# Attention values in eight blocks: two products a token group, halves joined by three engines

## The chip, the cores and the metric

The kernel runs on one core of a Trainium2 chip. A core has TensorE (PE in the profile; its weight loads are PEld), VectorE (DVE), ScalarE (ACT), GpSimd (POOL) and SyncE (SP), which only issues DMAs here. The metric is the device time of one launch in microseconds, the median of the runs shown; lower is better.

## The reference

Eight sequences of 1024 tokens and 256 channels pass through four sublayers, each followed by a residual and a layer norm. The third is the one that matters here: an attention in which each token attends over its own 16 heads.

```
q, k, v = qkv[..., :dh], qkv[..., dh:2*dh], qkv[..., 2*dh:]      # 16 heads of 16
scores = einsum('bnhd,bngd->bnhg', q, k) / 8
attn   = softmax(scores, axis=-1)
out    = einsum('bnhg,bngd->bnhd', attn, v)                      # the values
x      = out.reshape(b, n, -1) @ Wproj.T + bproj
```

The other sublayers are a linear attention with 1024 channels per sequence (a), a gated mixture of eight experts (the "moe" of a), and a feed-forward block on the 768 best tokens of each sequence (the router and ranking).

## The kernel before

The kernel is written engine by engine. Each engine has its own program, in which the order of the work is written out by hand in a function `turn(a, b, c)`; what one engine needs of another is a wait on a semaphore. A turn works on three sequences at once: a is in its first sublayer, b in the mixture of experts (`a_moe`, one call for each of eight token tiles), c in the head attention and the last sublayer. A turn lasts about 160 us. There are six turns with all three, at the start turns without c, and at the end one turn without a and one with c alone; so c's part runs eight times. An engine does its instructions strictly in the order of the turn.

Large numbers are kept as two fp16 parts, high (HI = 0) and low (LO = 1), with x = high + low. A product of two such numbers is the sum of three matmuls, `PASSES = ((HI, HI), (HI, LO), (LO, HI))`.

Tokens are handled in groups of eight (8 tokens x 16 channels of a head = 128 partitions). The matrix of one group is block-diagonal: `blockdiag` holds 128x128 fp16 weights for 16 groups and both parts. PE multiplies it with 16 columns. For the values (`b_o`) these columns are the transposed probabilities `probs_t`, which lie in the tile `ct`; the result of a group is 16 columns wide. Four steps q = 0 to 3 of 32 groups each fill a PSUM bank of 512 columns (O0 to O3). Per step PE does 32 x 3 = 96 matmuls, 384 a turn. PSUM banks for this part come from a ring of two (`b_bank`), so step q + 2 needs what step q left to be read.

After a step ScalarE rounds the bank to fp16 (the high part, 128x512, into `ohl`, which lies in the tile `stage`), and VectorE subtracts it from the bank (the low part, also into `stage`) and thereby frees the bank (`b_free`). When the last low part is there, SP and ScalarE issue four DMAs each to `scratch_o` in HBM; when all eight have landed SP issues two loads into `bt`, and from `bt` PE does the output projection (`b_pr`, weights `wproj`).

The order around it. On PE: `a_moe(b, 3)`, transposes of the probabilities (PT2, PT3), O0 to O3, then `a_tx(a, 0)`, `a_t(a, 0)`, `a_t(a, 1)`, `a_trow`, `a_tx(a, 1)`, `a_moe(b, 4)`, and then `b_pr(c, 0)`. On ScalarE: PT2, PT3, two block-diagonal copies (`b_spreadv(c, 1, ...)`), `a_moe(b, 3)` (four scaled copies), O0 to O3, `to_at_hi` of TX0, the stores of `b_storeo`, TX1. On VectorE: PT2, PT3, four block-diagonal products, O0 and O1, `a_moe(b, 3)` (four fused multiply-adds), O2 and O3, `a_tx(a, 0)`. On GpSimd: the scaling of the probabilities `b_s(c, 3)`, then `a_sum(b, 3)` (three additions) and the second layer norm's small steps.

Of the tile `prob` (128 x 2 x 512 fp32) nothing is needed once the last probabilities are transposed, until the router's scores.

## Time and profile before

| | |
|---|---|
| median of 3 runs | 1433.84 us (1431.96 to 1435.29) |
| the profiled execution | 1434.45 us, its span 1432.6 us |
| PE, PEld busy | 84%, 53% of the span |
| VectorE, ScalarE, GpSimd busy | 64%, 51%, 40% |
| mean granted TensorE clock | 0.855 of full speed |
| chain that ended last, by engine | PE 53%, DVE 18%, POOL 7%, issue 7%, DMA 6%, ACT 6% |

The chain is the work that set the end, followed back from the last instruction, step by step, to whatever released it. A wait of an engine counts only where that engine's next step lies on it.

### The profile page before, as it was taken

Reading aid. Unit: us, or ns where it says so; the run is one execution under the profiler, and the core shown is the slowest. Engines: PE = TensorE matmul, PEld = TensorE weight load, DVE = VectorE, ACT = ScalarE, POOL = GpSimd, SP = SyncE. Lnnn points to the kernel's source line nnn. Section 1 sums busy time; section 2 is a strip of 40 time slices with the busy share of each in tenths; the row PEclk is TensorE's granted clock in tenths of the full one; section 3 lists DMA queues with packets and bytes.
Section 4 is the critical chain, followed back from the end, with each engine's and each line's share of the span. In section 5 each row is a group of like instructions: output and inputs, shape, how many; then the busy total and the mean of one; then the engine's idle time right before and its main releaser. Section 6 shows DMA issues by size and latency. Waiting matters only on the chain.

```text
span 1432.6 us, 31148 instructions
## 1 busy us (share of the span) xinstructions
PE 1202.3 (84%) x12264; PEld 760.1 (53%) x12264; DVE 915.9 (64%) x2113; ACT 733.3 (51%) x1156; POOL 570.2 (40%) x887
## 2 busy tenths in 40 slices
PE   6689899997999899988999899988999898784443
PEld 3444456654665556654665556654665545442442
DVE  3534666587677866587677866587677776464534
ACT  3222465347554765357554675357454675356423
POOL 3125326425424525435424525435524515331312
PEclk8579998899879988899879987899879987787566
DMA  5000090205411190206410290207420290209220
GB/s 177 15 1 15 30 161 4 75 15 148 60 32 45 70 152 3 75 16 148 60 46 31 86 136 2 75 16 154 54 60 2 79 128 2 59 16 168 24 60 30
DMA packets 93145, 90.64 MB, mean 63 GB/s; under 512 B 7110, under 2 KB 81864, under 8 KB 92744
## 3 DMA queue, kind: packets, MB, share of 16 engines
q1 hardware_dynamic: 81736, 76.06, 26.8%
q0 software_dynamic: 2560, 8.39, 1.7%
q10 hardware_dynamic: 8704, 4.20, 1.1%
q8 instruction: 98, 1.61, 0.5%
q14 instruction: 47, 0.39, 0.1%
HBM read 46.68 MB, written 41.94 MB: 62 GB/s over the span
## 4 chain that ended last, share of the span: by engine, by line
PE 53%; DVE 18%; POOL 7%; issue 7%; DMA 6%; ACT 6%; SPq 2%; ACTq 1%; POOLq 0%; DVEq 0%
PE bank L1512 50%; DVE keys L1296 3%; POOL rs L521 2%; DVE x L1201 2%; DVE gelu L1298 2%; DVE stats L1060 2%; ACT x L793 1%; PE bank L1522 1%; DMA scratch_qkv<-part 1%; DMA scratch_qkv<-stage 1%; DMA bt<-scratch_o 1%; DVE ct L1030 1%; DMA scratch_o<-stage 1%; POOL stage L572 1%; DMA ct<-scratch_qkv 1%
## 5 line engine op out<-in xcount | busy, mean ns | idle before, releaser
L1512 PE MATMUL bank<-we,at 128*128 128x512 f16 x1536 | 365.5, 399 | 0.0
L1512 PEld LDWEIGHTS bank<-we,at 128*128 128x128 f16 x1536 | 154.0, 102 | 191.9 <-issue 36.4
L536 POOL TENSOR_TENSOR part<-part 128x512 f32<-128x512 f32 x64 | 83.0, 1297 | 353.8 <-ACTq L819 353.8
L671 ACT ACTIVATE part<-bank,wexp 128x256 f32<-128x256 f32 x256 | 105.2, 471 | 185.7 <-PE bank L1512 124.2
L1201 DVE SCALAR_TENSOR_TENSOR x<-bank,wexp,x 128x256 f32<-128x256 f32 x256 | 122.9, 480 | 81.0 <-PE bank L1512 75.0
L1512 PE MATMUL bank<-bt,wqkv 128*128 128x512 f16 x576 | 139.7, 385 | 15.6 <-DVE stage L1030 12.9
L793 ACT ACTIVATE x<-x,nm,rs 128x256 f32<-128x256 f32 x192 | 104.6, 593 | 92.5 <-POOL nm L524 91.2
L517 POOL TENSOR_SCALAR nm<-mv 128x2 f32<-128x2 f32 x128 | 32.3, 252 | 254.0 <-DVE mv L1065 248.5
L1030 DVE TENSOR_TENSOR stage<-bank,stage 128x512 f16<-128x512 f32 x112 | 75.6, 686 | 85.3 <-ACT stage L671 85.0
L1512 PE MATMUL bank<-keys,blockdiag 128*128 128x16 f16 x3072 | 96.6, 193 | 24.3 <-DMA keys<-scratch_qkv 18.5
L1512 PEld LDWEIGHTS bank<-keys,blockdiag 128*128 128x128 f16 x3072 | 95.6, 104 | 29.5 <-DMA keys<-scratch_qkv 19.0
L671 ACT ACTIVATE stage<-bank 128x512 f16<-128x512 f32 x112 | 66.2, 597 | 78.2 <-PE bank L1512 76.8
L1512 PE MATMUL bank<-ct,blockdiag 128*128 128x16 f16 x3072 | 82.9, 172 | 20.1 <-issue 20.0
L521 POOL TENSOR_TENSOR rs<-ve,half 128x2 f32<-128x2 f32 x128 | 95.3, 745 | 10.7
L1512 PEld LDWEIGHTS bank<-bt,wqkv 128*128 128x128 f16 x576 | 52.9, 99 | 83.9 <-DVE stage L1030 24.3
L1512 PEld LDWEIGHTS bank<-ct,blockdiag 128*128 128x128 f16 x3072 | 81.7, 101 | 22.6 <-issue 22.6
L1522 PE MATMUL bank<-const,x 128*128 128x128 f32 x384 | 59.6, 284 | 32.7 <-DVE ct L1030 15.9
L1030 DVE TENSOR_TENSOR ct<-bank,ct 128x512 f16<-128x512 f32 x64 | 41.6, 678 | 58.9 <-ACT ct L671 58.9
L671 ACT ACTIVATE blockdiag<-stage,const 128x2048 f16<-128x2048 f16 x40 | 78.1, 1994 | 0.0
L1060 DVE BATCH_NORM_STATS2 stats<-x 128x6 f32<-128x256 f32 x192 | 71.9, 416 | 8.7 <-POOL x L543 4.9
L572 POOL COPY stage<-ct 128x2048 f16<-128x2048 f16 x16 | 60.4, 3774 | 40.0 <-DMA ct<-scratch_qkv 39.9
L1522 PEld LDWEIGHTS bank<-const,x 128*128 128x128 f32 x384 | 45.7, 145 | 47.1 <-issue 21.5
(176 smaller groups left out, 2268.8 us busy)
## 6 DMA issues: line engine op xcount, KB each, us to landing
scratch_qkv<-stage SPq DMA_DIRECT2D x40, 512.0 KB, 3.8
ct<-scratch_qkv SPq DMA_DIRECT2D x128, 128.0 KB, 5.7
x_in<-in_x_dram SPq DMA_DIRECT2D x32, 256.0 KB, 2.7
keys<-scratch_qkv SPq DMA_DIRECT2D x64, 128.0 KB, 5.1
bt<-scratch_o SPq DMA_DIRECT2D x16, 512.0 KB, 3.7
out_dram<-x POOLq DMA_DIRECT2D x32, 256.0 KB, 2.7
scratch_qkv<-part SPq DMA_DIRECT2D x8, 512.0 KB, 8.2
scratch_o<-stage SPq DMA_DIRECT2D x32, 128.0 KB, 3.5
```

What stands on the lines that cost most here:

```text
L517: pool.tensor_scalar(nm[side][:, k, :], mv[side][:, k, :, 0], -1.0, None, ALU.mult)
L521: pool.tensor_tensor(rs[side][:, k, :], ve[side][:, k, :], half[:, 0:2], ALU.pow)\
L536: pool.tensor_tensor(part[:, 0:2, :], part[:, 0:2, :], part[:, 2:4, :], ALU.add)\
L572: pool.tensor_copy(v_rows[hf].rearrange("p (s c) h -> p s c h", c=8), compact[:, :, 8 * hf:8 * hf + 8, :]).then_inc(v_turned, 1)
L671: return act.activation(dst, src, ACT.Copy, scale=scale)
L793: ins = act.activation(dsts[t], srcs[t], ACT.Identity, bias=nm[side][:, k, t:t + 1], scale=rs[side][:, k, t:t + 1])
L1030: return dve.tensor_tensor(dst, src, hi, ALU.subtract)
L1060: ins = dve.bn_stats(stats[side][:, t, :], srcs[t])
L1201: ins = dve.scalar_tensor_tensor(out=dst, in0=m_bank[q][:, D * (e % 2):D * (e % 2 + 1)], scalar=wexp[:, t, e:e + 1], in1=dst, op0=ALU.mult ...
L1296: dve.tensor_scalar(beats_on[:, o:o + P * (T - 1 - t)], scores[:, P * (t + 1):C], me, None, ALU.is_le, ALU.add, accum_out=rowsum[:, t, 0:1])
L1512: ins = pe.matmul(dst, lhs, rhs, start=(n == 0), stop=(n == len(terms) - 1))
L1522: ins = pe.transpose(ps[:, 2 * P * k + P * t:2 * P * k + P * (t + 1)], src[:, 2 * p + t, P * k:P * (k + 1)], ident)
```

## The change

The bank of a step is now filled by 16 groups instead of 32, and a group takes two matmuls instead of three: one of the high weights with high and low probabilities together (32 columns), and one of the low weights with the high probabilities (16 columns), which adds to the first 16 of those. A group's result so lies in PSUM as two halves of 16 columns that have still to be added. There are eight steps n (O0 to O7) of 32 matmuls and 512 PSUM columns each.

The halves are joined in four steps. ScalarE copies the LO half (256 columns) from PSUM into one of four places in `prob` (`b_oextra`). VectorE adds the other half to it from PSUM, in place, and frees the bank (`b_o`). ScalarE rounds the sum to fp16 from `prob` into `ohl` (`b_o`). GpSimd subtracts that from the sum and writes the low part (`b_olo`). From n = 4 on ScalarE's first copy also waits for GpSimd to have read the place. The stores wait for GpSimd's eighth step.

On VectorE `a_moe(b, 3)` now stands between steps 3 and 4; on ScalarE copy n comes ahead of rounding n - 1; on GpSimd the eight steps stand ahead of `a_sum(b, 3)`.

```diff
-        def o_part(q, part):
-            return ohl[:, :, part, :].rearrange("p h (r c) -> p h r c", c=16)[:, :, :, 4 * q:4 * q + 4]
-
-        def o_psum(q):
-            return b_ps(f"O{q}").rearrange("p (c r h) -> p h r c", c=4, r=T)
+        def o_part(n, part):
+            return ohl[:, :, part, :].rearrange("p h (r c) -> p h r c", c=16)[:, :, :, 2 * n:2 * n + 2]
+
+        def o_products(n):
+
+            return b_ps(f"O{n}").rearrange("p (a l g) -> p l a g", l=2, g=H)
+
+        def o_half(n):
+            return prob[:, n // 2 % 2, 256 * (n % 2):256 * (n % 2 + 1)]
+
+        def o_sum(n):
+            return o_half(n).rearrange("p (c r h) -> p h r c", c=2, r=T)
...
-                sp.wait_ge(b_free[b_ring("O2")], b_read(b, "O2"))
-                sp.sem_inc(waits_held, 1)
-                sp.wait_ge(b_free[b_ring("O3")], b_read(b, "O3"))
+                sp.wait_ge(o_lo, 8 * (b + 1))
...
+            def b_olo(b, n):
+                pool.wait_ge(o_hi, 8 * b + n + 1)
+                pool.sem_inc(waits_held, 1)
+                pool.tensor_tensor(o_part(n, LO), o_sum(n), o_part(n, HI), ALU.subtract).then_inc(o_lo, 1)
...
                     b_s(c, 3)
+                    for n in range(8):
+                        b_olo(c, n)
                 if b is not None:
                     a_sum(b, 3)
                     ln(b, 5, 0)
...
-            def b_o(b, q):
-                act.wait_ge(b_full, b_filled(b, f"O{q}"))
+            def b_oextra(b, n):
+                act.wait_ge(b_full, b_filled(b, f"O{n}"))
+                if n >= 4:
+                    act.wait_ge(o_lo, 8 * b + n - 3)
+                copy(o_half(n).rearrange("p (a g) -> p a g", g=H), o_products(n)[:, LO]).then_inc(o_extra, 1)
+
+            def b_o(b, n):
+                act.wait_ge(b_free[b_ring(f"O{n}")], b_read(b, f"O{n}"))
                 for hf in range(2):
                     act.wait_ge(v_spread[hf], 2 * (b + 1))
-                copy(o_part(q, HI), o_psum(q)).then_inc(o_hi, 1)
+                copy(o_part(n, HI), o_sum(n)).then_inc(o_hi, 1)
 
             def b_storeo(b):
-                for q in (2, 3):
-                    act.wait_ge(b_free[b_ring(f"O{q}")], b_read(b, f"O{q}"))
-                    act.sem_inc(waits_held, 1)
+                act.wait_ge(o_lo, 8 * (b + 1))
+                act.sem_inc(waits_held, 1)
...
-                    b_o(c, 0)
-                    b_o(c, 1)
-                    b_o(c, 2)
-                    b_o(c, 3)
+                    b_oextra(c, 0)
+                    for n in range(1, 8):
+                        b_oextra(c, n)
+                        b_o(c, n - 1)
+                    b_o(c, 7)
...
-            def b_o(b, q):
-                dve.wait_ge(o_hi, 4 * b + q + 1)
-                split_lo(o_part(q, LO), o_psum(q), o_part(q, HI)).then_inc(b_free[b_ring(f"O{q}")], 1)
+            def b_o(b, n):
+                dve.wait_ge(o_extra, 8 * b + n + 1)
+                half = o_half(n).rearrange("p (a g) -> p a g", g=H)
+                dve.tensor_tensor(half, o_products(n)[:, HI], half, ALU.add).then_inc(b_free[b_ring(f"O{n}")], 1)
...
                     b_spreadv(c, 1, range(2, 6), last=True)
-                    b_o(c, 0)
-                    b_o(c, 1)
+                    for n in range(4):
+                        b_o(c, n)
                 if b is not None:
                     a_moe(b, 3)
                 if c is not None:
-                    b_o(c, 2)
-                    b_o(c, 3)
+                    for n in range(4, 8):
+                        b_o(c, n)
...
-            def b_o(b, q):
-                pe.wait_ge(v_spread[q // 2], 2 * (b + 1))
-                pe.wait_ge(b_free[b_ring(f"O{q}")], b_before(b, f"O{q}"))
-                pe.wait_ge(b_free[1 - b_ring(f"O{q}")], b_other(b, f"O{q}", (f"PT{q}",)))
-                for c in range(4):
+            def b_o(b, n):
+                pe.wait_ge(v_spread[n // 4], 2 * (b + 1))
+                pe.wait_ge(b_free[b_ring(f"O{n}")], b_before(b, f"O{n}"))
+                pe.wait_ge(b_free[1 - b_ring(f"O{n}")], b_other(b, f"O{n}", (f"PT{n // 2}",)))
+                for c in range(2):
                     for r in range(T):
-                        n = T * c + r
-                        ins = sum_of(b_ps(f"O{q}")[:, H * n:H * (n + 1)],
-                                     [(block(q, i, r, c),
-                                       probs_t[:, j, 4 * q + c, H * r:H * (r + 1)]) for i, j in PASSES])
+                        o, m = 2 * H * (T * c + r), 2 * n + c
+                        seen = probs_t[:, :, m, H * r:H * (r + 1)]
+                        pe.matmul(b_ps(f"O{n}")[:, o:o + 2 * H], block(HI, r, m), seen, start=True, stop=False)
+                        ins = pe.matmul(b_ps(f"O{n}")[:, o:o + H], block(LO, r, m), seen[:, HI, :],
+                                        start=False, stop=True)
                 ins.then_inc(b_full, 1)
 
             def b_pr(b, p):
```

## Rows read from the trace of the kernel before

**Rows 1.** Timeline of one of six full turns: start us, us, engine, line, work [idle]

```profile
568.82 3.89 ACT L671 ACTIVATE blockdiag<-stage,const 128x2048 f16<-128x2048 f16 x2
...
569.27 5.01 PE L1512 MATMUL bank<-ct,blockdiag 128*128 128x16 f16 x192 [1.02 <-issue]
...
572.60 1.56 ACT L671 ACTIVATE part<-bank,wexp 128x256 f32<-128x256 f32 x4
...
574.36 1.08 ACT L671 ACTIVATE stage<-bank 128x512 f16<-128x512 f32 x2 [0.19 <-PE bank L1512]
574.99 1.29 DVE L1030 TENSOR_TENSOR stage<-bank,stage 128x512 f16<-128x512 f32 x2 [2.58 <-ACT stage L671]
...
575.78 3.96 PE L1512 MATMUL bank<-ct,blockdiag 128*128 128x16 f16 x143 [1.51 <-issue]
576.20 2.03 DVE L1201 SCALAR_TENSOR_TENSOR x<-bank,wexp,x 128x256 f32<-128x256 f32 x4
...
581.57 0.60 ACT L671 ACTIVATE stage<-bank 128x512 f16<-128x512 f32 x1 [2.45 <-PE bank L1512]
...
582.20 0.69 DVE L1030 TENSOR_TENSOR stage<-bank,stage 128x512 f16<-128x512 f32 x1 [2.35 <-ACT stage L671]
...
582.52 0.60 ACT L671 ACTIVATE at<-bank 128x512 f16<-128x512 f32 x1 [0.35 <-PE bank L1522]
582.99 3.17 SPq L454 DMA_DIRECT2D scratch_o<-stage  x4
...
588.90 5.34 PE L1512 MATMUL bank<-we,at 128*128 128x512 f16 x24
...
594.09 0.55 PEld L1512 LDWEIGHTS bank<-wproj,bt 128*128 128x128 f16 x6 [0.34 <-DMA bt<-scratch_o]
```

**Rows 2.** Windows of it: stretch, us, busy PE PEld DVE ACT POOL, clock, DMA

```profile
569.27:574.30 5.03, 5.01 (x192) 4.91 (x192) 3.15 (x5) 4.90 (x6) 0.01 (x1) 0.93 0.01 3
575.80:581.50 5.70, 5.36 (x193) 5.29 (x194) 3.01 (x6) 0.60 (x1) 1.30 (x2) 0.50 0.03 6
```

**Rows 3.** Timeline, first projection work: six full turns (first, last), then the seventh

```profile
273.52 0.55 PEld L1512 LDWEIGHTS bank<-wproj,bt 128*128 128x128 f16 x6 [0.74 <-DMA bt<-scratch_o]
...
1075.24 0.57 PEld L1512 LDWEIGHTS bank<-wproj,bt 128*128 128x128 f16 x6 [0.29 <-DMA bt<-scratch_o]
...
1232.11 1.46 PE L1512 MATMUL bank<-wproj,bt 128*128 128x256 f16 x6 [6.13 <-DMA bt<-scratch_o]
```

**Rows 4.** Timeline of the last turn, in which c is alone

```profile
1356.39 10.43 PE L1512 MATMUL bank<-ct,blockdiag 128*128 128x16 f16 x384 [2.07 <-issue]
...
1359.65 0.60 ACT L671 ACTIVATE stage<-bank 128x512 f16<-128x512 f32 x1 [0.56 <-DVE blockdiag L1228]
...
1367.49 0.69 DVE L1030 TENSOR_TENSOR stage<-bank,stage 128x512 f16<-128x512 f32 x1 [1.87 <-ACT stage L671]
...
1379.17 1.25 PE L1512 MATMUL bank<-wproj,bt 128*128 128x256 f16 x5 [12.35 <-DMA bt<-scratch_o]
```

**Rows 5.** Groups by line and shape: busy us, mean ns of one, idle before

```profile
L671 ACT ACTIVATE blockdiag<-stage,const 128x2048 f16<-128x2048 f16 x40 | 78.1, 1994 | 0.0
...
L572 POOL COPY stage<-ct 128x2048 f16<-128x2048 f16 x16 | 60.4, 3774 | 40.0 <-DMA ct<-scratch_qkv 39.9
...
L539 POOL TENSOR_TENSOR part<-part 128x256 f32<-128x256 f32 x64 | 47.3, 739 | 5.0
...
L530 POOL TENSOR_TENSOR xs<-x_in,xs 128x512 f16<-128x512 f32 x32 | 36.1, 1156 | 54.3 <-ACT xs L671 54.2
...
L671 ACT ACTIVATE shared<-ct 128x2048 f16<-128x2048 f16 x8 | 29.8, 3719 | 0.0
...
L565 POOL COPY x<-x 128x512 f32<-128x512 f32 x32 | 19.5, 612 | 7.6 <-DMA out_dram<-x 7.5
...
L1111 DVE TENSOR_TENSOR shared<-bank,iq 128x256 f32<-128x256 f32 x8 | 3.3, 417 | 0.0
...
L671 ACT ACTIVATE iq<-bank 128x256 f32<-128x256 f32 x8 | 3.1, 384 | 20.6 <-PE bank L1512 20.6
```

More of the change, by code:

```diff
@@ L38, in build_two_layer_postln @@
               "F10", "F11", "S0", "S1", "PT0", "S2", "PT1", "S3", "PT2", "PT3", "O0", "O1", "O2", "O3",
+              "O4", "O5", "O6", "O7",
               "PR0", "PR1", "PR2", "PR3", "TZ0", "TZ1", "TZ2", "TZ3", "ROUT0", "ROUT1", "SCOL0",
@@ L213, in build_two_layer_postln @@
         pt_hi = sem("pt_hi")
+        o_extra = sem("o_extra")
         o_hi = sem("o_hi")
+        o_lo = sem("o_lo")
         o_stored = sem("o_stored")
@@ L1658, in b_f, with block @@
                     .then_inc(b_full, 1)
-            def block(q, part, t, c):
-                return blockdiag[:, q // 2, 64 * part + 8 * t + 4 * (q % 2) + c, :]
+            def block(part, t, m):
+                return blockdiag[:, m // 8, 64 * part + 8 * t + m % 8, :]
             def b_s(b, q):
@@ L1673, in b_s @@
                         ins = sum_of(b_ps(f"S{q}")[:, H * n:H * (n + 1)],
-                                     [(block(q, i, g, c), keys[:, :, P * j + token])
+                                     [(block(i, g, 4 * q + c), keys[:, :, P * j + token])
                                       for i, j in PASSES])
@@ L1770, in turn @@
                     b_pt(c, 3)
-                    b_o(c, 0)
-                    b_o(c, 1)
-                    b_o(c, 2)
-                    b_o(c, 3)
+                    for n in range(8):
+                        b_o(c, n)
                 if b is None and c is None:
```

## The prediction

> **What bounds the kernel now.** I first looked at the granted clock and at the chain that ended last, which runs mostly through PE. The value products fill their stretch, so fewer of them look like time won. Whether that is so is decided by what starts the output projection, the first thing that needs the values. The timeline of a full turn answers it. PE begins the values at 569.27 and does 192 matmuls in 5.01 us, then stands until 575.78, because ScalarE is still busy with its block-diagonal copies (from 568.82) and with the four scaled copies of the experts (572.60 to 574.16), and reads the first bank only at 574.36 [rows 1]. The last low part ends at 582.20 + 0.69 = 582.89, the stores go out at 582.99, and the projection's first weights load at 594.09, 11.1 us later, after a wait of 0.34 us for the loads of `bt` [rows 1]. So the projection waits for DMA, not for PE, and the expert matmuls in front of it (5.34 us from 588.90 [rows 1]) just cover the transfers. It is the same in every turn: in the six full ones the wait is between 0.29 and 0.74 us (I show the first and the last), in the seventh, which has no a, it is 6.13 us [rows 3]; in the last nothing stands in front but the transfers. The end is therefore set, in all eight turns, by the moment at which the last low part of the values is in `stage`. PE's own time in the values is not what is late.
>
> **PE: 384 matmuls become 256.** The 192 matmuls take 26.1 ns each at a mean granted clock of 0.93, and 143 of the later ones 3.96 us, 27.7 ns each, in a stretch at 0.50, which is the 1.2 GHz level [rows 1, 2]. In the last turn 384 take 10.43 us, 27.2 ns each [rows 4]. The rate hardly follows the clock, so the 16 columns are not what limits them, and I take 27.4 ns also for the 32-column product: a step of 32 matmuls is 0.88 us. That removes 128 x 27.4 ns = 3.5 us of PE a turn, 28 us in all. No row has a 32-column product. Its bounds are 27.4 ns, and twice that if the columns counted, with the other half unchanged, which makes 1.3 us a step.
>
> **Prices of the joining.** ScalarE's copy of a half from PSUM is like the 128x256 copy of `iq`, 0.384 us; VectorE's addition is like the 128x256 product from PSUM, 0.417 us [rows 5]. ScalarE's rounding reads `prob` in jumps of 512 bytes, then 64. Nearest is its copy out of `ct`, in jumps of 256 bytes: 3719 ns against 1994 ns for as many elements read in a row, 0.84 ns more an element [rows 5]. With 256 elements that is 0.2 us on 0.4: I take 0.60, bounds 0.40 and 0.60. GpSimd's subtraction is bounded below by half of its 128x512 one to fp16, 1156 / 2 = 0.58 us; the nearest whole row is 0.739 us for 128x256 [rows 5]. It too reads in jumps: its copy out of `ct` takes 3774 / 2048 = 1.84 ns an element, the straight one 612 / 512 = 1.20, so 0.64 x 256 = 0.16 us more for one such operand and 0.33 for two [rows 5]. I take 0.74 + 0.16 = 0.90, bounds 0.58 and 1.10. Handing over costs 0.03 us from ScalarE to VectorE (582.17 to 582.20) and 0.10 from VectorE to PE or to a DMA issue (582.89 to 582.99) [rows 1].
>
> The same jumps are weighed by a rule. The Trainium skill, GPSIMD Engine Reference, section "Performance pitfalls for Q7 kernels", says that reading SBUF with steps above 8 bytes costs some 2.9 instead of 1.9 cycles an element; at its 1.2 GHz this is an estimate of 0.21 us for 256 elements. GpSimd would then take 0.95 us and the whole sum below would be 17.4 us instead of 16.2. It speaks against giving this work to GpSimd.
>
> **A full turn, step by step** (times on the clock of [rows 1]).
> Steps 0 and 1 are through PE at 571.0, since only their two banks are free. ScalarE does not come before 574.36: nothing of its work ahead of that is changed. It copies half 0 until 574.75 and half 1 until 575.05 (independent ones overlap a little, as the pair in 1.08 us shows [rows 1]). VectorE's first addition ends at 575.20, and PE resumes at 575.3, only 0.5 us earlier than now, with six of its eight steps still to do, where now it has half.
> From there the round PE, ScalarE, VectorE, PE paces it: step 2 ends at 576.2, 3 at 577.1, 4 at 578.1, 5 at 579.0. VectorE ends addition 3 at 578.0 and then does the experts' four operations, 2.03 us [rows 1], before addition 4 (580.4). The banks of 4 and 5 are held for that time; PE does step 6 from 580.5 and step 7 until 582.3, 0.7 us later than now.
> Then the tail: copy 7 until 582.7, addition until 583.2, rounding until 583.8. GpSimd's subtraction 6 runs from 583.3 to 584.2 and 7 until 585.1. Against 582.89 that is +2.25 us. Behind bank 7 there was one rounding and one subtraction, now there are four steps on three engines. The transfers take their 11.1 us as before, so the projection starts 2.25 us later. PE, which arrives 0.7 us later, is hidden by that.
> With the bounds it is +1.4 us (0.40 and 0.58) to +2.85 us (0.60 and 1.10).
>
> **What is queued behind the new waits.** On ScalarE, TX0 moves from 582.52 to about 583.8; PE's T0 matmuls, which do not need it, cover that. ScalarE's issue of stores waits for GpSimd with TX1 behind it, which PE delivers only after 588, so nothing is lost. On GpSimd, `a_sum(b, 3)` goes behind the eight subtractions: from 585.1, with additions of about 1.16, 0.74 and 0.74 us [rows 5], it ends near 587.9, and VectorE wants it for the norm's statistics after the T work, just about then; the cost is nothing as long as the subtractions end before 586, and after that VectorE's wait runs beside the transfers. SP's x loads go out behind the stores, 2 us later, for use in the next turn.
>
> **The seventh turn** has the same order, +2.25. **The last** has no expert work: PE is now continuous for 10.43 us from 1356.39, ScalarE is idle from 1359.09, and the end is 1367.49 + 0.69 = 1368.18 [rows 4]. With halves from 1359.1, additions from 1359.6 and a round of about 0.95 us a step, step 7 is through PE at 1365.7, 1.1 us earlier; the tail of 2.9 us ends at 1368.6: +0.4 (bounds -0.4 and +1.6).
>
> **Sum.** 7 x 2.25 + 0.4 = 16.2 us; bounds 7 x 1.4 - 0.4 = 9.3 and 7 x 2.85 + 1.6 = 21.6. After the projection every engine keeps its order and is behind it, so I take nothing back. The profiled execution took 1434.45 us, 0.6 above the median, so 1434.45 + 16.2 - 0.6 = 1450.
>
> **The rivals.**
> *PE's time is the gain.* If the projection followed PE's last value matmul, 8 x 3.5 = 28 us would go: 1406. For it speaks that PE is most of the chain; against it that the projection waits for DMA in all turns [rows 3] and that ScalarE reads nothing before 574.36. It decides from the point at which ScalarE's first copy comes before about 571.5, and nothing moves it there. Chance 0.04; a part of it, with a gain of over 3 us, 0.02.
> *No difference.* Later in the turn some wait that does not stem from c takes up the delay. At the lower bound, with most of it taken up, the result is 1434 to 1437. I saw no such wait. Chance 0.08.
> *GpSimd paces.* If one subtraction takes 1.3 us or more, eight of them from 575.9 end at 586.3, +3.4 a turn and +3.0 in the last: 1434 + 27 = 1461. Two operands in jumps point that way, the rows up to 1.1 do not reach it. A 32-column product at 1.3 us a step gives 3.9 a turn and 2.6 in the last, +30: 1464. Together 0.12.
> *The clock falls in the longer wait before the projection.* In the seventh turn, after 6.13 us of waiting, its first six matmuls take 1.46 us [rows 3]; were it so in the six full turns, over 1 us more each, near 1458. There PE would wait for some 1.8 us only. Chance 0.06.
> *The forecast*, 1443 to 1456: chance 0.68.
>
> **How the numbers follow.** The likeliest is 1450. The range, 1440 to 1461, holds the forecast, the clock's case, half of the pacing case and what lies between the forecast and no difference. A difference of about 0.2% (2.9 us) is what a measurement of this kernel can tell from none. Faster 0.06, same 0.08, slower 0.86.
>
> **What would show it.** Right: PE idle for over 4 us after 64 value matmuls; ScalarE's first half at the place of today's first rounding; stores some 2 us later after the start of the values, and the projection's wait for `bt` grown from 0.3 to about 1.8 us in full turns. Wrong: a subtraction on GpSimd outside 0.58 to 1.10 us, a step of PE over 1 us, a rounding from `prob` at 0.4 us (which takes 0.2 off a turn), or a projection that starts without waiting for its load.

## The result

The changed kernel takes 1459.48 us (median of 4 runs, 1454.47 to 1462.97), the kernel before beside it 1432.9 us (1430.16 to 1435.29): a ratio of 1.0183, 95% interval 1.0142 to 1.0225. The sign is as forecast; the size, 26 us, is not the 16 us of the sum. 1459 lies above the forecast's own 1443 to 1456, just inside the upper edge of the range of 1440 to 1461. The profiled execution took 1456.38 us with a span of 1454.6 us, 22.0 us more than the span before, at a mean granted clock of 0.864 (before 0.855).

The page of the kernel after: span, busy time by engine, and the chain that ended last.

```profile
span 1454.6 us, 29436 instructions
...
PE 1172.2 (81%) x11240; PEld 734.0 (50%) x11240; DVE 923.8 (64%) x2145; ACT 772.7 (53%) x1252; POOL 635.6 (44%) x951
...
PE 46%; DVE 17%; issue 10%; POOL 9%; DMA 8%; ACT 6%; SPq 2%; ACTq 1%; POOLq 0%; DVEq 0%
```

PE's share of the chain fell from 53% to 46%, while issue, GpSimd and DMA took its place. PE has less to do and waits more.

The groups of the changed value stage, by line and shape: count, busy us, mean ns of one, idle before and what ended it.

```profile
L592 POOL TENSOR_TENSOR stage<-prob,stage 128x256 f16<-128x256 f32 x64 | 62.0, 988 | 93.1 <-ACT stage L686 92.8
...
L686 ACT ACTIVATE stage<-prob 128x256 f16<-128x256 f32 x64 | 41.5, 657 | 9.0 <-DVE prob L1288 9.0
...
L1288 DVE TENSOR_TENSOR prob<-bank,prob 128x256 f32<-128x256 f32 x64 | 25.8, 422 | 44.2 <-ACT prob L686 43.1
L686 ACT ACTIVATE prob<-bank 128x256 f32<-128x256 f32 x64 | 23.7, 383 | 9.4 <-PE bank L1717 8.6
```

The copy (383 ns) and the addition (422 ns) cost what their nearest rows of before did, 384 and 417 [rows 5]. The two operations that read `prob` in jumps cost more than I took: 657 ns for the rounding against 600, 988 ns for the subtraction against 900, though this one is inside its bounds.

The timeline of the same full turn as in [rows 1], after: start us, us, engine, line, work, idle before. PE's rows come in pairs of lines for 32 and 16 columns; the first of a run stands.

```profile
574.32 0.18 PE L1716 MATMUL bank<-ct,blockdiag 128*128 128x32 f16 x1 [1.02 <-issue]
...
577.65 1.56 ACT L686 ACTIVATE part<-bank,wexp 128x256 f32<-128x256 f32 x4
...
579.33 0.66 ACT L686 ACTIVATE prob<-bank 128x256 f32<-128x256 f32 x2
...
580.27 0.19 PE L1716 MATMUL bank<-ct,blockdiag 128*128 128x32 f16 x1 [4.20 <-issue]
...
582.92 2.03 DVE L1222 SCALAR_TENSOR_TENSOR x<-bank,wexp,x 128x256 f32<-128x256 f32 x4
...
587.59 0.38 ACT L686 ACTIVATE prob<-bank 128x256 f32<-128x256 f32 x1
...
587.85 2.85 POOL L592 TENSOR_TENSOR stage<-prob,stage 128x256 f16<-128x256 f32 x3 [0.48 <-ACT stage L686]
...
588.00 0.42 DVE L1288 TENSOR_TENSOR prob<-bank,prob 128x256 f32<-128x256 f32 x1 [0.43 <-ACT prob L686]
...
590.80 3.26 SPq L462 DMA_DIRECT2D scratch_o<-stage  x4
...
601.88 0.55 PEld L1534 LDWEIGHTS bank<-wproj,bt 128*128 128x128 f16 x6 [0.97 <-DMA bt<-scratch_o]
```

From the first value matmul to the first store this turn takes 590.80 - 574.32 = 16.48 us; before it took 582.99 - 569.27 = 13.72 [rows 1]. Read down: PE does its two banks and then stands 4.20 us (before 1.51 [rows 1]), because ScalarE first does the scaled copies of the experts; the experts on VectorE at 582.92 hold the banks of steps 4 and 5; and the last copy at 587.59 is followed by an addition (588.00) and a rounding, while GpSimd does the last three subtractions in a row from 587.85 on, the last of which ends at 590.70.

Put together over all eight turns, from both timelines:

| | before | after | difference, us |
|---|---|---|---|
| first value matmul to first store, seven turns, sum | 93.4 | 115.1 | +21.7 |
| the same in the last turn | 11.88 | 12.65 | +0.8 |
| first store to projection, eight turns, sum | 90.2 | 92.2 | +2.0 |
| projections, sum | 53.8 | 58.6 | +4.8 |
| from a projection to the next turn's values, and before the first | | | -7.4 |
| span | 1432.6 | 1454.6 | +22.0 |

In this sum the stage itself gives all of it, +3.1 us a turn. The projections' +4.8 us and the -7.4 us nearly cancel, and 1.8 us of the latter lie before the first value matmul of the program, where nothing was changed. The section on the prediction comes back to both.

### The profile page after: what moved, and what is told of

Read it like the earlier page. It is cut to its first block, busy times and chain, and to the rows that moved or that the text cites. A ratio compares the mean times of both kernels' runs of the same rounds, so it can differ in the third digit from the quotient of the medians.

```text
span 1454.6 us, 29436 instructions
## 1 busy us (share of the span) xinstructions
PE 1172.2 (81%) x11240; PEld 734.0 (50%) x11240; DVE 923.8 (64%) x2145; ACT 772.7 (53%) x1252; POOL 635.6 (44%) x951
## 4 chain that ended last, share of the span: by engine, by line
PE 46%; DVE 17%; issue 10%; POOL 9%; DMA 8%; ACT 6%; SPq 2%; ACTq 1%; POOLq 0%; DVEq 0%
PE bank L1534 41%; DVE keys L1318 3%; PE bank L1716 2%; POOL rs L529 2%; DMA bt<-scratch_o 2%; DMA scratch_o<-stage 2%; DVE x L1222 2%; DVE gelu L1320 2%; ACT x L813 1%; POOL stage L592 1%; DVE stats L1081 1%; ACTq L783 1%; DVE ct L1051 1%; DMA scratch_qkv<-part 1%; DMA scratch_qkv<-stage 1%
## 5 line engine op out<-in xcount | busy, mean ns | idle before, releaser
L1534 PE MATMUL bank<-bt,wqkv 128*128 128x512 f16 x576 | 137.5, 380 | 16.6 <-DVE stage L1051 13.7
L592 POOL TENSOR_TENSOR stage<-prob,stage 128x256 f16<-128x256 f32 x64 | 62.0, 988 | 93.1 <-ACT stage L686 92.8
L1716 PE MATMUL bank<-ct,blockdiag 128*128 128x32 f16 x1024 | 58.4, 185 | 52.2 <-issue 51.1
L1544 PE MATMUL bank<-const,x 128*128 128x128 f32 x384 | 59.7, 285 | 32.7 <-DVE ct L1051 16.2
L1534 PE MATMUL bank<-wproj,bt 128*128 128x256 f16 x384 | 57.7, 300 | 33.8 <-DMA bt<-scratch_o 33.8
L1716 PEld LDWEIGHTS bank<-ct,blockdiag 128*128 128x128 f16 x1024 | 55.8, 102 | 55.6 <-issue 55.6
L1051 DVE TENSOR_TENSOR stage<-bank,stage 128x512 f16<-128x512 f32 x80 | 54.2, 685 | 40.2 <-ACT stage L686 40.0
```

The source lines that it names most:

```text
L592: pool.tensor_tensor(o_part(n, LO), o_sum(n), o_part(n, HI), ALU.subtract).then_inc(o_lo, 1)
L1051: return dve.tensor_tensor(dst, src, hi, ALU.subtract)
L1534: ins = pe.matmul(dst, lhs, rhs, start=(n == 0), stop=(n == len(terms) - 1))
L1544: ins = pe.transpose(ps[:, 2 * P * k + P * t:2 * P * k + P * (t + 1)], src[:, 2 * p + t, P * k:P * (k + 1)], ident)
L1716: pe.matmul(b_ps(f"O{n}")[:, o:o + 2 * H], block(HI, r, m), seen, start=True, stop=False)
```

## The experiments

The change has three parts: steps of a quarter of the work that a bank held before (eight half-filled blocks instead of four), two matmuls a group instead of three, and the joining of the halves. The first two experiments take the parts one by one; the others test which neighbour of the stage makes it slow. "Stage" below is the time from the first value matmul to the first store in a full turn: 13.2 to 13.7 us before, 16.4 to 16.5 after. The rows shown are those of the third full turn, as above.

**Only the smaller blocks.** Three products of 16 columns a group as before, in eight steps; ScalarE rounds each half bank, VectorE subtracts. Nothing is left out.

```
def o_first(n):
    return b_ps(f"O{n}")[:, 0:256].rearrange("p (c r h) -> p h r c", c=2, r=T)
# ScalarE
copy(o_part(n, HI), o_first(n)).then_inc(o_hi, 1)
# VectorE
split_lo(o_part(n, LO), o_first(n), o_part(n, HI)).then_inc(b_free[b_ring(f"O{n}")], 1)
```

> Block size alone: the three products of the kernel before (384 matmuls a turn) in eight steps of 16 groups, ScalarE rounding and VectorE subtracting 256 columns straight from PSUM; VectorE's expert operations between steps 3 and 4 as in the changed kernel. Nothing is left out. Theory 1: a step is 1.32 us of PE, only two steps (not half the work) are done when ScalarE arrives, and VectorE's expert operations hold two banks, so the stores go out 15.3 to 15.8 us after the first value matmul (before 13.2, without the joining 14.3): about 1449, so that the block size alone costs more than two thirds of what the change cost. If block size is harmless, 13.2 to 13.6 and 1434 to 1437.

Measured: 1461.51 us (1460.49 to 1467.44), ratio 1.0217 [1.0181, 1.0252]. The stage takes 15.99 us in every full turn and 13.33 in the last. Timeline of its PE, ScalarE, VectorE and ScalarE's queue:

```profile
575.24 2.56 PE L1521 MATMUL bank<-ct,blockdiag 128*128 128x16 f16 x96 [1.02 <-issue]
...
590.28 0.40 ACT L682 ACTIVATE stage<-bank 128x256 f16<-128x256 f32 x1 [0.87 <-PE bank L1521]
...
590.71 0.42 DVE L1039 TENSOR_TENSOR stage<-bank,stage 128x256 f16<-128x256 f32 x1 [0.85 <-ACT stage L682]
...
591.38 3.48 ACTq L774 DMA_DIRECT2D scratch_o<-stage  x4
```

The tail behind PE is short, 590.28 to 591.13, and yet the whole loss is there. The cause is in front: two banks now hold a quarter of the values instead of half, so PE does 96 of its 384 matmuls, a quarter, before it must wait for a late ScalarE (the first row; before it did 192 [rows 1]), and its value part lasts 15.0 us. I had priced this too low: 15.3 to 15.8 us for the stage and about 1449 in all. PE's value part, 3.2 us longer than before, also brings PE to the projection as late as the loads: its weight loads wait only 0.12 to 0.40 us there in five of the six full turns. The smaller block alone costs as much as the whole change does.

**Two products, no joining.** The low-probability half of each product is left out of the values; `o_first` is then the first half of the products; ScalarE rounds it straight from PSUM, VectorE subtracts, GpSimd has nothing to do here.

```
# ScalarE
copy(o_part(n, HI), o_first(n)).then_inc(o_hi, 1)
# VectorE
split_lo(o_part(n, LO), o_first(n), o_part(n, HI)).then_inc(b_free[b_ring(f"O{n}")], 1)
```

> PE's part of the change without the joining: the same 256 matmuls in eight steps, but ScalarE rounds the first half straight from PSUM and VectorE subtracts it there, as before; the half with the low probabilities is left out of the values. Theory 1 (the stores wait for ScalarE's arrival and for the chain behind the last bank, PE's time in the values is not on the path): from the first value matmul to the stores 13.3 to 14.0 us, as before (13.2), time within +0 to +6 us of the kernel before. Theory 2 (PE's saved 3.5 us a turn count and the joining hides them): about 9.8 us to the stores and 1405 us.

Measured: 1443.26 us (1442.82 to 1446.28), ratio 1.0043 [1.0028, 1.0059]. The stage takes 14.3 us, a little over the 13.3 to 14.0 expected, and 11.10 in the last turn. Timeline, PE, VectorE and SP's queue:

```profile
574.31 0.18 PE L1703 MATMUL bank<-ct,blockdiag 128*128 128x32 f16 x1 [1.02 <-issue]
...
588.12 0.43 DVE L1039 TENSOR_TENSOR stage<-bank,stage 128x256 f16<-128x256 f32 x1 [0.42 <-ACT stage L682]
...
588.64 3.54 SPq L465 DMA_DIRECT2D scratch_o<-stage  x4
```

The three kernels give the parts: in a full turn the stage goes from 13.3 to 16.0 us by the smaller blocks, back to 14.3 by the two products, and up to 16.4 by the joining; in the whole time that is +26, -18 and +16 us by the medians, and about +31, -25 and +20 us by the ratios to the runs of the kernel before beside each. The two products do give something once the steps are small, but that pays back only two thirds to four fifths of what the small steps cost. Even with the joining free, the kernel is not faster than before.

**The changed kernel once more**, beside the same runs of the kernel before as the smaller blocks:

> The changed kernel once more, beside the same runs of the kernel before: 1.014 to 1.022 of it, stores 16.4 us after the first value matmul. It shows how far single executions of the same program lie apart.

Measured: 1457.28 us (1455.65 to 1460.48), ratio 1.0176 [1.0151, 1.0202]. The stage takes 16.40 to 16.46 us in the full turns.

**GpSimd's subtraction on VectorE.** It tests whether GpSimd, the slowest of the three in the tail, is what costs.

```
# VectorE; GpSimd's loop of b_olo is gone
def b_olo(b, n):
    dve.wait_ge(o_hi, 8 * b + n + 1)
    split_lo(o_part(n, LO), o_sum(n), o_part(n, HI)).then_inc(o_lo, 1)
...
b_o(c, n)
b_olo(c, n - 1)
```

> The changed kernel with the low part subtracted by VectorE instead of GpSimd. Theory 1: the last subtraction costs 0.45 us behind the last rounding instead of 1.5, so the stores go out 1.0 to 1.2 us earlier after the first value matmul (16.4 to about 15.3), some 8 us less than the changed kernel, 1449 to 1453. If GpSimd's share is hidden, 16.4 stays and so does the time.

Measured: 1457.42 us, ratio 1.0137 [1.0112, 1.0163], against 1.0176 [1.0151, 1.0202] for the changed kernel; the intervals overlap. Timeline: PE's first value matmul, the last two subtractions, SP's stores.

```profile
578.08 0.18 PE L1722 MATMUL bank<-ct,blockdiag 128*128 128x32 f16 x1 [1.02 <-issue]
...
593.20 1.22 DVE L1049 TENSOR_TENSOR stage<-prob,stage 128x256 f16<-128x256 f32 x2
594.51 3.17 SPq L462 DMA_DIRECT2D scratch_o<-stage  x4
```

Its group:

```profile
L1049 DVE TENSOR_TENSOR stage<-prob,stage 128x256 f16<-128x256 f32 x64 | 42.5, 664 | 6.1 <-ACT stage L684 3.1
```

One subtraction takes 664 ns instead of 988, and the last turn's stage is 0.76 us shorter (11.89). In the full turns nothing is gained: the stage takes 594.51 - 578.08 = 16.43 us, since VectorE's additions, which free PE's banks, now stand behind subtractions, and PE needs 14.1 us for the values instead of 13.2. What the tail won the steps lost. GpSimd's price matters only where VectorE has time.

**ScalarE's halves ahead of its expert copies.** This takes away the late arrival that the forecast named as what makes PE's saving worthless. `a_moe(b, 3)` is done after TX0's rounding instead.

```
-                if b is not None:
-                    a_moe(b, 3)
                 if c is not None:
                     b_oextra(c, 0)
...
+                if b is not None:
+                    a_moe(b, 3)
```

> The changed kernel with ScalarE's four scaled copies of the experts moved from ahead of the value steps to behind them (between TX0 and the stores). Theory 1: ScalarE reads the first half 1.6 us earlier, and the stores go out 1.6 us earlier (16.4 to 14.8): 11 us less than the changed kernel, about 1447. If VectorE's four expert operations or GpSimd pace the steps, less than 0.5 us a turn comes of it.

Measured: 1448.31 us, ratio 1.0075 [1.0055, 1.0094]. Timeline of PE, ScalarE and SP's queue:

```profile
572.96 0.18 PE L1716 MATMUL bank<-ct,blockdiag 128*128 128x32 f16 x1 [1.02 <-issue]
...
576.30 0.65 ACT L686 ACTIVATE prob<-bank 128x256 f32<-128x256 f32 x2
...
587.76 3.40 SPq L462 DMA_DIRECT2D scratch_o<-stage  x4
```

ScalarE's first halves come 3.34 us after PE's start instead of 5.01, and the stage takes 14.80 us instead of 16.48: what was moved (1.56 us of copies) comes off the stage in full. The time falls by 9 us, less than seven times that, and not evenly over the turns, as the section on the prediction shows.

**The same in the kernel before.** `a_moe(b, 3)` on ScalarE goes between the roundings 1 and 2. It tests whether this order is something that the change brings, or was to be had before.

```
-                if b is not None:
-                    a_moe(b, 3)
...
                 # after b_o(c, 1), ahead of b_o(c, 2)
+                if b is not None:
+                    a_moe(b, 3)
```

> The kernel before with the same four scaled copies moved from ahead of the value steps to between the second and the third. Theory 1: the stores go out 1.5 us earlier in the seven turns that have them (13.2 to 11.7), about 10 us less than before, 1422 to 1425, unless PE, which arrives only 0.3 us ahead of the loads, becomes the bound; it comes 1.5 us earlier too, since its third step waits for ScalarE. Theory 2 (PE's work in the values is the bound): no change.

Measured: 1427.95 us (1427.31 to 1428.88), ratio 0.9936 [0.9916, 0.9956]: faster than before. Timeline of PE, ScalarE and SP's queue:

```profile
565.78 10.45 PE L1513 MATMUL bank<-ct,blockdiag 128*128 128x16 f16 x384 [1.19 <-issue]
...
569.34 0.60 ACT L671 ACTIVATE stage<-bank 128x512 f16<-128x512 f32 x1
...
577.69 3.15 SPq L454 DMA_DIRECT2D scratch_o<-stage  x4
```

In this turn PE does all 384 matmuls without a pause, in 10.45 us, as it does in the last turn of before, 10.43 us [rows 4]. The stage takes 11.7 to 12.4 us in the full turns, 1.4 us less on average. Of this 7 us in all reach the span, and not evenly: from one turn's values to the next the second full turn is 2.8 us shorter, the third 0.6 and the seventh turn 3.4, the other full turns not at all. In the first and the fifth the transfers took 12.9 and 13.1 us instead of 11.6, in the second PE came to the projection 0.8 us after the loads, and in the other three within 0.4 us ahead of them.

**VectorE's additions ahead of its expert work.** The second holding point: the four fused multiply-adds of `a_moe(b, 3)` go behind all eight additions.

```
-                    for n in range(4):
+                    for n in range(8):
                         b_o(c, n)
                 if b is not None:
                     a_moe(b, 3)
-                if c is not None:
-                    for n in range(4, 8):
-                        b_o(c, n)
```

> The changed kernel with VectorE's four expert operations (2.03 us) moved from between additions 3 and 4 to behind addition 7. Theory 1: PE's steps 6 and 7 no longer wait for them, the stores go out 0.6 to 0.8 us earlier after the first value matmul (16.4 to 15.7), about 5 us less than the changed kernel. If GpSimd's subtractions (0.99 us each) pace the steps by now, the gain is under 0.3 us a turn.

Measured: 1450.21 us, ratio 1.0101 [1.0065, 1.0138]. Timeline of PE, GpSimd and SP's queue:

```profile
573.99 0.18 PE L1713 MATMUL bank<-ct,blockdiag 128*128 128x32 f16 x1 [1.08 <-issue]
...
582.07 6.86 POOL L592 TENSOR_TENSOR stage<-prob,stage 128x256 f16<-128x256 f32 x7 [0.39 <-ACT stage L686]
...
589.03 3.24 SPq L462 DMA_DIRECT2D scratch_o<-stage  x4
```

The stage takes 15.04 us, 1.4 less. It stops there because GpSimd now does seven subtractions without a pause (6.86 us, 0.98 each): here, once VectorE is out of the way, GpSimd paces, as one of the rivals had it.

**Work in PE's wait.** The page of after shows PE waiting for `bt` ahead of the projection. Half of the next expert tile (12 matmuls 128x512, about 2.67 us) is moved into that wait. It also tests whether the clock, which falls around that wait in some turns, costs time of its own.

```
# PE: def a_moe(a, t, qs=range(4)); after a_moe(b, 4), ahead of b_pr(c, 0)
+                    a_moe(b, 5, range(0, 2))
...
-                    a_moe(b, 5)
+                    a_moe(b, 5, range(2, 4))
```

> The changed kernel with the first half of PE's expert matmuls of tile 5 (12 of 24, 2.67 us) moved from behind the projection to ahead of it, into PE's wait for the loads. Theory 1 with its clock part (the projection is late by the longer transfer chain, PE waits 0.5 to 3.4 us for it, and after waits over 2 us the projection runs at the lower clock level, 7.95 instead of 6.28 us): the wait is used, 1.3 to 1.9 us a full turn, and all projections of the full turns take 6.3 us: 12 to 16 us less than the changed kernel, 1443 to 1447. If the wait before the projection is not what the change lost, the time stays or rises by what the projection is held back.

Measured: 1443.42 us (1440.92 to 1444.78), ratio 1.0054 [1.0037, 1.0070]: 14 us off the changed kernel by the medians, 12.9 us off its span. The stage is unchanged (16.4 to 16.5 us). The waits that the moved work could use sum to 13.1 us: 1.24, 2.32, 0.49, 2.67 of 3.36, 1.56 and 2.17 in the six full turns and 2.67 of 8.4 in the seventh. The sums agree, but the turns do not: from one turn's values to the next these seven turns became shorter by 0.1, 3.4, 3.3, 3.7, 2.9, 0.7 and 1.0 us. The third, with the shortest wait, gained 3.3 us; the first, with 1.24, gained nothing. So filling the wait wins the time, but not as the length of each wait, and the agreement of the sums is luck. Timeline, PE's weight loads:

```profile
592.23 7.54 PEld L1534 LDWEIGHTS bank<-we,at 128*128 128x128 f16 x36
599.89 0.75 PEld L1534 LDWEIGHTS bank<-wproj,bt 128*128 128x128 f16 x6
```

In this turn there is no wait at the projection any more; in the six full turns the weight loads wait 0.12 to 1.45 us (after 0.97 to 3.84), and none has a projection of 7.6 us or more, where after had three. What each of the two is worth this run can't tell.

**All three moves on the changed kernel.**

> The changed kernel with all three moves: ScalarE's scaled copies behind the steps, VectorE's expert operations behind them, half of expert tile 5 ahead of the projection. Theory 1: stores 14.0 to 14.3 us after the first value matmul, PE's wait used up, so that PE's own arrival decides, which is 0.3 to 0.8 us earlier than in the kernel before: 1428 to 1434. Theory 2 would have PE's 28 us show up here: 1410 or less.

Measured: 1426.8 us (1421.98 to 1430.96), ratio 0.9946 [0.9926, 0.9966]: faster than before. Timeline of PE, GpSimd and SP's queue:

```profile
566.12 0.18 PE L1713 MATMUL bank<-ct,blockdiag 128*128 128x32 f16 x1 [1.08 <-issue]
...
572.52 6.95 POOL L592 TENSOR_TENSOR stage<-prob,stage 128x256 f16<-128x256 f32 x7 [0.38 <-ACT stage L686]
...
579.57 3.18 SPq L462 DMA_DIRECT2D scratch_o<-stage  x4
```

The stage takes 13.45 us, of which GpSimd's row of seven is half, less than the 14.0 to 14.3 expected and about as long as before. The projection starts 25.6 to 26.6 us after the values in the full turns, where before it started after 24.5 to 24.8, but with half an expert tile more done by then.

**The kernel before, with two of the moves.** ScalarE first and the wait filled, no part of the change.

> The kernel before with ScalarE's scaled copies between the second and the third step, as in the run above, and with half of expert tile 5 ahead of the projection. There PE waits 0 to 1.2 us for the loads in the full turns, so the second move can give 2 us in all beyond the first: 1422 to 1427; and if the extra work ahead of the projection holds it back without need, up to 5 us more than with the first move alone.

Measured: 1425.05 us (1423.34 to 1427.21), ratio 0.9926 [0.9900, 0.9953], the fastest time here. Timeline of PE:

```profile
568.55 10.25 PE L1513 MATMUL bank<-ct,blockdiag 128*128 128x16 f16 x384 [1.02 <-issue]
...
587.21 7.93 PE L1513 MATMUL bank<-we,at 128*128 128x512 f16 x36
```

PE goes from its values (10.25 us without a pause) through the longer expert work (36 matmuls instead of 24 in front of the projection) without waiting. The interval overlaps that of the kernel above. So with its neighbours set right the change is worth nothing that can be told here, in either direction: what the two kernels win, they win by the moved neighbours. VectorE's move was not tried on the kernel before.

**The moves and the subtraction on VectorE.** GpSimd paces the combined kernel, so its share goes to VectorE.

> The changed kernel with the three moves and the low part by VectorE instead of GpSimd. GpSimd's seven subtractions in a row (0.99 us each) paced the version with three moves, whose stores went out at 13.4 us. Here VectorE has 0.42 + 0.61 us a step: about 1.0 to 1.1 us a step and 0.6 us behind the last rounding instead of 1.6, so the stores at 12.6 to 13.2 us. PE's arrival is what decides in the full turns there, so at most 2 to 4 us less than 1427; the same time if the steps take 1.1 us.

Measured: 1431.59 us (1428.13 to 1434.32), ratio 0.9980 [0.9963, 0.9998], slower than the combined kernel by 5 us, with intervals that just overlap. Timeline of PE, SP's queue and VectorE:

```profile
566.21 0.18 PE L1721 MATMUL bank<-ct,blockdiag 128*128 128x32 f16 x1 [1.02 <-issue]
...
578.85 2.48 SPq L462 DMA_DIRECT2D scratch_o<-stage  x4
...
580.85 0.69 DVE L1049 TENSOR_TENSOR at<-bank,at 128x512 f16<-128x512 f32 x1
```

The stores do go out 0.8 us sooner after PE's start (12.64 us against 13.45). But VectorE gets to the tile TX0 later, and PE's next expert work, which waits for what is made from it, begins 19.5 us after the start of the values instead of 18.3. PE was already last at the projection, so this delay reached it and the gain did not: the projection starts 27.2 us after the values in this turn, against 26.0.

## Why the prediction was right in sign and low in size

**What starts the projection: right, by a small margin.** Before, the loads of `bt` came last in every full turn, as I read from the weight loads' waits of 0.29 to 0.74 us. But PE was then just ending its last matmuls: its own idle time at the projection was 0.25 us in the first full turn, 0.1 in the fifth and none in the others. So stores that go out earlier would soon have met PE, unless it came earlier too, while later ones, as here, delay the projection in full. The projection waited for `bt` in all full turns of after, 0.49 to 3.36 us on PE, and in the seventh 8.4. Of PE's saving, 3.5 us a turn by its own work, the two products shortened the stage by 1.7 us (16.0 to 14.3) and only against small steps; the rest stood beside other waits. That ScalarE's arrival is one of these was tested by moving it, and the stage followed by the full 1.7 us.

**The schedule of the steps: right.** In the turn that I worked out, PE resumed 5.95 us after its start (forecast 6.0), after an idle time of 4.20 us, and ScalarE, the ends of steps 2 to 5 and the experts' hold on VectorE came within about 0.1 us of the schedule. Step 7 and with it the last copy ended 0.2 us later than scheduled. The 32-column product costs what the 16-column one does; the starts of two steps in a row lie 0.80 us apart at full clock and 0.85 at the lower level, where I had taken 0.88.

Windows of after: stretch, us, busy PE PEld DVE ACT POOL, clock, DMA share, GB/s. The first two are the beginnings of projections, of the second turn and of the turn shown; the third is of the steps behind the pause; the last is of PE's next work (T0) in the turn shown.

```profile
438.00:440.00 2.00, 1.73 (x10) 1.32 (x11) 0.00 (x0) 0.04 (x1) 1.66 (x3) 0.64 0.52 181
601.90:603.90 2.00, 2.00 (x19) 1.80 (x20) 0.27 (x1) 1.47 (x4) 1.42 (x2) 1.00 0.49 171
...
580.30:582.00 1.70, 1.70 (x64) 1.70 (x64) 0.48 (x2) 1.24 (x3) 0.97 (x1) 0.50 0.04 10
...
589.10:592.10 3.00, 3.00 (x5) 1.35 (x4) 0.84 (x2) 0.50 (x2) 2.92 (x4) 0.50 0.10 15
```

64 matmuls, half of them with 32 columns, take 1.70 us at a clock of 0.50: 26.6 ns each.

**The size of a turn: low, by three mis-sized terms.** The sum had 16.2 us; the stores came 22.5 us later. Of the difference of 6.3 us:

- The tail, some 3.6 us. The subtraction took 0.99 us, not 0.90, and three of them stood in a row at the end, so the error counted several times; with 0.2 us from the last copy the last subtraction ended 0.5 us later than scheduled, in seven turns. The Trainium skill, GPSIMD Engine Reference, section "Performance pitfalls for Q7 kernels", from which the prediction drew an estimate of 0.95 us, was nearer to the measured 0.988 than my row-based 0.90.
- The turn I compared with, some 2.4 us. I read one turn and multiplied by seven. It was the longest of before: its stage took 13.72 us, with a pause of PE of 0.34 us in it, one other took 13.52 and five took 13.22 to 13.24. After had no such spread (16.40 to 16.48). The difference was therefore 3.1 us on average, not 2.76.
- The last turn, 0.4 us: +0.8 instead of +0.4, by the same tail.

The rounding at 657 ns lay outside its upper bound of 0.60; its 0.06 us is part of the tail. It reads fp32 in steps of 512 bytes; the bound came from fp16 in steps of 256 bytes in `ct`. Which of the two makes it dearer no run shows.

**After the stores: right on balance, with two parts that I did not see.** The sum took nothing for what follows; measured is -0.5 us (+2.0, +4.8, -7.4). The 11.1 us of transfers varied between 11.05 and 12.44. That the other two nearly cancel is luck, as far as the runs show.

**A turn's length moves in jumps: not foreseen.** From the first value matmul of a full turn to that of the next, us, in the first five full turns (the sixth is followed by a turn without a):

| kernel | stage | 1 | 2 | 3 | 4 | 5 |
|---|---|---|---|---|---|---|
| before | 13.2 to 13.7 | 160.3 | 160.3 | 160.5 | 160.4 | 160.5 |
| after | 16.4 to 16.5 | 163.5 | 163.9 | 163.7 | 164.2 | 163.5 |
| `small_three` | 16.0 | 163.5 | 163.9 | 163.9 | 163.9 | 163.8 |
| `no_join` | 14.3 | 163.6 | 160.5 | 160.7 | 163.4 | 163.9 |
| `scalar_first` | 14.7 to 14.8 | 164.0 | 160.2 | 160.5 | 163.7 | 163.8 |
| `vector_late` | 15.0 to 15.1 | 163.8 | 160.4 | 160.3 | 160.4 | 164.0 |
| `wait_filled` | 16.4 to 16.5 | 163.5 | 160.5 | 160.4 | 160.5 | 160.6 |
| `combined` | 13.4 to 13.5 | 160.3 | 157.3 | 160.1 | 157.3 | 160.1 |

With the same stage a turn is either about 160.4 or about 163.7 us long (in `combined` about 157.3 or 160.2), and in none of the thirteen traces does one of these turns lie between 157.6 and 159.9 or between 160.7 and 163.4. So a shorter stage shows in the time by the number of turns that jump, not by its own length in each. In after all five turns are of the longer kind, +3.2 us on average, which is close to the stage's +3.1. My sum adds a delay turn by turn and has no such step; what a stage longer by its 2.25 us would have given is not shown. What causes the jumps was not tested; the clock, next, goes with them.

**The clock rival: it occurred; its cost stays open.** It was given 0.06 and 1458. The granted clock fell again ahead of the projections of the second, fourth and sixth full turns; the first of these projections took 7.95 us against 6.28 in the turns without it. Timeline of the second and the fourth turns, the projection's first row:

```profile
438.26 0.72 PEld L1534 LDWEIGHTS bank<-wproj,bt 128*128 128x128 f16 x6 [2.80 <-DMA bt<-scratch_o]
...
766.90 0.99 PEld L1534 LDWEIGHTS bank<-wproj,bt 128*128 128x128 f16 x6 [3.84 <-DMA bt<-scratch_o]
```

In after these waits are the longer ones; in the turn shown in full, with 0.97 us, the clock was 1.00 at the projection. The length of the wait does not settle it, though: in `after_again` the fifth full turn waited 2.82 us and kept the clock at 1.00, and in the second, with 2.88, it fell to 0.50. Within after the turns with slow projections are no longer than the others: from the start of a projection to the next turn's values it is 136.1 and 135.3 us in the second and fourth, and 135.4, 136.1 and 135.0 in the first, third and fifth. But those others had the lower level elsewhere: in the turn shown T0's work runs at 0.50 (the last window above), where before it ran at 1.00. Window of before, as long after the first value matmul as that one:

```profile
584.05:587.05 3.00, 3.00 (x9) 0.94 (x8) 1.78 (x3) 0.00 (x0) 0.00 (x0) 1.00 0.93 201
```

So up to the end of its projection each full turn of after has some 3 us more at the lower level than before has, at one place or the other. Other kernels show what a turn without either looks like. Timeline of `vector_late`, the projection's first row in its fourth and fifth full turns:

```profile
760.36 0.55 PEld L1531 LDWEIGHTS bank<-wproj,bt 128*128 128x128 f16 x6 [1.48 <-DMA bt<-scratch_o]
...
922.87 0.98 PEld L1531 LDWEIGHTS bank<-wproj,bt 128*128 128x128 f16 x6 [3.61 <-DMA bt<-scratch_o]
```

The fourth is 160.4 us long and the fifth 164.0, with equal stages to 0.1 us: 2.0 us of the difference are longer transfers and 1.6 the slow projection, and of both only 0.2 us comes back behind it. In this kernel and in `scalar_first` all five long turns have a slow projection and none of the five short ones has. In the table's rows from after to `wait_filled` every turn of the longer kind has the lower level once more at one of the two places, and of the shorter ones only the third of `no_join` has. That is a coincidence in time, not yet a cause: the longer transfers come with it, and no run changes the clock alone. So the measured 1459 speaks neither for this rival nor against it, and the clock's share in the time was not separated from the stage's.

**What is queued behind the new waits: half right.** PE was to arrive at the projection 0.7 us later. In the second and fourth turns it did: the expert tile's weight loads ended 25.1 us after the start of the values (27.86 less the wait of 2.80, for the second) against 24.5 before. In the turn shown it ended at 26.6, for there the clock came back from 0.50 some 3 us later in the turn than before, and the T0 work ran longer at that level. In both cases the load of `bt` came last, so it stayed hidden.

**GpSimd paces: not in this kernel.** It had pauses of 1.00 and 0.48 us in the turn shown. It paces in `vector_late` and `combined`, where the work ahead of it was moved away.

**PE's time is the gain: no.** `small_three` and `no_join` show how much of it is: a third of PE's value work gone is worth 18 to 25 us where the steps are small, and less than the small steps cost.

## What to carry to other kernels

Cutting a step in half while the ring keeps its number of banks halves the work that a producer can do ahead of a late consumer; work out how much is buffered at the moment when the consumer arrives, before counting what the cut saves. When fewer matmuls are bought with more steps on slower engines, follow the last block through all of them, since that tail, not the sum, is added. And take a difference over all turns, not from one: here a turn with a chance pause hid a tenth of the loss. When the sum of a run agrees with a sum of waits, compare them turn by turn as well: in `wait_filled` the sums agreed and the turns did not. The cheaper gain lay in the order of the neighbours: the kernel before gained 0.6% when one engine did its unrelated copies two steps later.

## What the runs showed of the hardware

- A 32-column fp16 product with its weight load costs what a 16-column one does, at both levels of the clock: 64 matmuls, half of each kind, took 1.58 us at 1.00 (2.4 GHz), the row below, or 24.7 ns each, and 1.70 us at 0.50 (1.2 GHz), shown above, or 26.6 ns; with 16 columns alone it is 24.8 and 26.4 ns, by the next two rows. Window of after:

```profile
574.30:575.90 1.60, 1.58 (x64) 1.60 (x64) 1.60 (x3) 1.60 (x2) 0.00 (x0) 1.00 0.00 0
```

- The clock fell while PE was busy without a pause. In the fastest kernel, the one of before with two moves, PE starts its 384 small matmuls at full clock, and 4.4 us later the rest runs at 0.50 with PE busy for all of 5.60 us. Windows of that kernel:

```profile
568.60:572.60 4.00, 4.00 (x161) 4.00 (x162) 3.10 (x5) 3.89 (x3) 0.00 (x0) 1.00 0.01 4
573.00:578.60 5.60, 5.60 (x212) 5.56 (x209) 3.66 (x7) 2.65 (x6) 2.67 (x3) 0.50 0.02 6
```

The Trainium skill, TensorE: Matmul & The Clock Gate, section "What's actually happening", has the default state throttled and activity releasing it, with the lower level for an idle array. The rows do not agree with that as it stands: here PE's row shows no idleness, as far as the profile's modelled ends of matmuls can show it, and the clock is at its lower level. For matmuls as small as these it hardly matters, as the two rows show: 24.8 ns a matmul at 1.00 and 26.4 at 0.50.

- Reading fp32 from SBUF in steps is dear on ScalarE and VectorE, from PSUM it is not; GpSimd's reading is slower by as much, though its output type differs too. For 128x256 elements: ScalarE's rounding takes 657 ns from `prob` in steps of 512 bytes, 405 ns from a PSUM bank in the same steps (`small_three`, below), and its fp32 copy out of PSUM in runs of 16 elements 383 ns; VectorE's subtraction takes 664 ns from `prob` and 0.42 us from PSUM in the same steps (`small_three`); GpSimd's takes 988 ns against 739 for an addition in a row [rows 5]. Group of `small_three`:

```profile
L682 ACT ACTIVATE stage<-bank 128x256 f16<-128x256 f32 x64 | 25.0, 405 | 58.8 <-PE bank L1521 56.9 <-ACT part L682 1.4 <-DVE blockdiag L1237 0.6
```

The Trainium skill, Advanced Engine Details and Errata, section "SBUF Cachelines", says that an access in another cacheline each time pays a penalty. The 657 ns agree with it for SBUF; for ScalarE's read of PSUM, 405 against 383 ns, these runs show next to none.
